# Second layer's selective scan: the input load split in two, dt's sum and u's product moved to GpSimd, the chain that makes u started two groups earlier

## The chip, the core and the metric

The kernel runs on one core of a Trainium2 chip. The metric is the device time of one launch in microseconds (us). Five engines work side by side, each through its own list of instructions: TensorE (PE, with its weight loads shown as PEld), VectorE (DVE), ScalarE (ACT), GpSimd (POOL) and SyncE (SP), which here only issues DMAs. They order themselves by semaphores.

## The reference, cut to what matters

Two layers on an input of 4 images x 128 channels x 64 x 64. Layer 0 is attention with a layer norm; the change does not touch it. Layer 1 adds a 3x3 convolution, a 1x1 convolution between a Fourier transform and its inverse, and a Mamba block over the 4096 positions of each image:

```python
xi, z = split(u @ in_proj)                       # 256 channels each
xs = silu(causal_conv1d(xi, 4 taps) + conv1d_b)
x_dbl = xs @ x_proj.T                            # 8 (for dt) + 16 (B) + 16 (C)
dt = softplus(x_dbl[:8] @ dt_proj.T + dt_proj_b)
h  = exp(dt * A) * h + dt * B * xs               # 256 channels x 16 states
y  = sum_over_states(h * C) + xs * D
ym = (y * silu(z)) @ out_proj.T
out = conv3x3(x) + irfft2(mix(rfft2(x))) + ym
```

## The kernel before

Layer 0 leaves its output in `z_ext` in memory, with a halo of 64 zeros on both sides of each image. Layer 1 (`layer1`) cuts the 4 x 4096 positions into 32 iterations (`NIT`) of 512 positions. In an iteration the 4096 pairs of channel and state are 32 groups (`G`) of 128 rows, and each group is one scan of 128 x 512. The first two iterations are unrolled; the other 30 are 15 passes of a hardware loop (L848) whose body holds two iterations. SyncE's list is unrolled throughout.

There is no scheduler. Each engine has an `emit(it, p)`, which goes through the groups g = 0 to 31 of iteration `it`, and a `prepare(j, p, g)`, which puts a piece of the preparation of the next iteration j = it + 1 behind the work of group g. The numbers in `if g == ...` set where each piece stands in its engine's list. An engine meets them when it comes there, and waits there if the semaphore isn't up.

For each group:

- SP (`load_dt`, L884) loads the group's dt rows from memory, each row repeated for 16 states, into one of 16 buffers `d_a`, when the scan 16 groups earlier is done. It reads them from `dt_dram`, to which `store_dt` (L878) has written the iteration's dt; `store_dt` stands at t = 16 of SP's list and waits for `dt_sum`.
- ACT (`decay`, L1113) makes exp(dt A) in place; `last_state` (L1106) keeps the last state of group g - 6, so ACT is at most six groups ahead of the scans.
- PE (`repeat_u`, L1016) spreads u = dt x over 128 rows into one of four banks; it waits for the scan four groups back, so PE is at most that far ahead.
- DVE multiplies the bank by B (`times_b`, L1181, one group ahead) and scans (L1195). The scan waits for POOL to be done with the state buffer of eight groups earlier.
- POOL multiplies the states by C (`hc`, L1224), and PE sums four groups of them over the states (`sum_states`, L999).

Twice an iteration DVE adds the skip term (`add_skip`, L1166, at g = 21 and, for the iteration before, g = 5) and POOL multiplies by the gate (L1215).

The preparation: `load` brings the 512 positions with their halo to `za` (for the taps, the gate and the Fourier part), the same again to a padded image `zp` (for the 3x3 convolution), and the mirrored rows to `stage_j`. All three count on the semaphore `z_in`, and PE's taps (L935, g = 1 to 7) and ACT's flip (L1066, g = 3) wait for all of them. `load(it + 2)` stands at t = 26 of SP's list and waits for `z_used`, which PE raises when it has used `zp` and `zj` of iteration `it`, the last of the output products of `fill` (at g = 28). From the taps follow silu (g = 10), `xd` (PE g = 11 and 12, ACT g = 15), dt's product (PE g = 15 and 16), Relu and Abs (ACT g = 19 and 20), Exp and Ln (g = 21 and 22, semaphore `sp_log`); then on DVE the sum dt (L1154, g = 20) and the product ux = dt xs (L1157, g = 21, semaphore `u_prod`), then ACT's `high` (L1059) and DVE's `low` (L1148, g = 25 and 26), which split ux into two parts that add up to it, as PE's fast number format needs.

The code that the change touches is printed here with the line numbers of the profile.

Of the kernel before, what the change touches and what calls it, by code (L numbers as in the profile page):

```python
# [8 lines left out]
ALU = mybir.AluOpType  # L9
AX = mybir.AxisListType  # L10

B, C, H, W = 4, 128, 64, 64
# [664 lines left out]
LC = 512  # L677
# [7 lines left out]
def layer1(nc, z_ext, w, out, nb=B):  # L685
# [16 lines left out]
    with ExitStack() as ctx:  # L702
# [59 lines left out]
        with nc.Block() as block:  # L762
# [27 lines left out]
            def _(dve):  # L790
# [23 lines left out]
        (z_in, flipped, item, item_read, sp_log, dt_sum, u_prod, hi_ready, lo_ready,  # L814
         u_rep, da_ready, bu_ready, scanned, kept, hc_ready, y_done, y_added, gated, z_used, o_ready, o_copied,
         o_full, o_even, o_odd, dt_stored) = [sem(x) for x in (
             "z_in", "flipped", "item", "item_read", "sp_log", "dt_sum", "u_prod",
# [35 lines left out]
        with nc.Block() as block:  # L853
            @block.sync
            def _(sp):
                def load(j, p):

                    jw = j % NIT
                    b, lc = jw // STEPS, jw % STEPS

                    ge(sp, z_used, j - 1)
                    ge(sp, flipped, 2 * j)
                    sp.dma_start(za[:, p, :], z_ext[b, :, bass.ds(lc * LC, HALO)]).then_inc(z_in, 16)
                    sp.dma_start(zp[:, p, :, 1:W + 1], z_ext[b, :, bass.ds(lc * LC, HALO)].rearrange("c (h w) -> c h w", w=W)).then_inc(z_in, 16)
# [3 lines left out]
                    sp.dma_start(stage_j[:, ROWS - 1, :], z_ext[b, :, bass.ds((STEPS - lc) % STEPS * LC + W, W)]).then_inc(z_in, 16)  # L868

# [17 lines left out]
                def emit(it, p):  # L887
                    for t in range(G):
# [10 lines left out]
                        if t == 26 and it + 2 <= NIT:  # L899
                            load(it + 2, p)  # L900

                load(0, 0)
                load(1, 1)
# [11 lines left out]
                sp.wait_ge(z_in, 64 * (NIT + 1))  # L915

            @block.tensor
            def _(pe):
# [7 lines left out]
                def prepare(j, p, g):  # L926

                    if 1 <= g <= 7:
                        if g == 1:
                            pe.wait_ge(z_in, j * 64 + 64)  # L930
# [8 lines left out]
                    elif g in (11, 12):  # L939
                        i = g - 11  # L940
# [7 lines left out]
                    elif g in (15, 16):  # L948
                        n = DT + g - 15
# [3 lines left out]
                        nc.tensor.matmul(bank(n), wdt[:, 128 * (g - 15):128 * (g - 15) + 128], xd[:, :], start=True, stop=True  # L953
                                         ).then_inc(item, 1)
                    elif g in (19, 20):
                        n = BI + g - 19
                        begin(j, n)
                        nc.tensor.matmul(bank(n), (sel_b, sel_c)[g - 19][:, :], xd[:, :], start=True, stop=True).then_inc(item, 1)
# [59 lines left out]
                FILLS = (18, 21, 21, 24, 24, 25, 26, 27, 27, 28)  # L1018

                def emit(it, p):  # L1020
                    for g in range(G):
# [4 lines left out]
                        if g in (13, 14) and not (isinstance(it, int) and it == 0):  # L1026
                            out_proj(it - 1, g - 13)
# [283 lines left out]
```

## Time and profile before

| | |
|---|---|
| median of 3 runs | 6187.24 us (6182.13 to 6188.05) |
| profiled execution | 6181.0 us, span 6179.2 us |
| layer 1's scans, first start to last start | 4006.8 to 6163.3 us of the span |
| busy over the span | PE 90%, DVE 79%, POOL 67%, ACT 60% |
| busy from 4006 to 6164 us | DVE 2022.24, PE 1659.10, POOL 1495.03, ACT 1328.44 of 2158 us |

The last row is the one to read: the shares over the whole span mix two layers. The profiled execution is one run; its times are used for sums, and the medians for comparison.

### The profile page before, as it was taken

Reading aid. Unit: us, or ns where it says so; the run is one execution under the profiler, and the core shown is the slowest. Engines: PE = TensorE matmul, PEld = TensorE weight load, DVE = VectorE, ACT = ScalarE, POOL = GpSimd, SP = SyncE. Lnnn points to the kernel's source line nnn. Section 1 sums busy time; section 2 is a strip of 40 time slices with the busy share of each in tenths; the row PEclk is TensorE's granted clock in tenths of the full one; section 3 lists DMA queues with packets and bytes.
Section 4 is the critical chain, followed back from the end, with each engine's and each line's share of the span. In section 5 each row is a group of like instructions: output and inputs, shape, how many; then the busy total and the mean of one; then the engine's idle time right before and its main releaser. Section 6 shows DMA issues by size and latency. Waiting matters only on the chain. (4 is left out here: it accounts for less than half of the span.)

```text
span 6179.2 us, 90944 instructions
## 1 busy us (share of the span) xinstructions
PE 5589.3 (90%) x27184; PEld 2550.2 (41%) x27184; DVE 4912.2 (79%) x7188; ACT 3717.1 (60%) x7290; POOL 4118.1 (67%) x3147
## 2 busy tenths in 40 slices
PE   7999999999999999999999999677777777777777
PEld 3444444444444444444444444233333333333332
DVE  7777777777777777777777777299999999999998
ACT  3666666666656666666666666566566656666665
POOL 2677766676766677666677776376676666676776
PEclk9999999999999999999999999899899889988998
DMA  4011011111110110110100000244444444444444
GB/s 132 20 42 40 29 31 34 32 43 30 32 35 25 38 42 29 40 33 23 31 18 12 21 9 21 67 164 144 157 150 143 153 151 148 142 157 149 146 153 144
DMA packets 293852, 465.18 MB, mean 75 GB/s; under 512 B 73680, under 2 KB 97104, under 8 KB 291920
## 3 DMA queue, kind: packets, MB, share of 16 engines
q1 hardware_dynamic: 293360, 459.70, 23.4%
q8 instruction: 177, 2.90, 0.2%
q14 instruction: 315, 2.58, 0.1%
HBM read 381.74 MB, written 76.28 MB: 74 GB/s over the span
## 5 line engine op out<-in xcount | busy, mean ns | idle before, releaser
L560 POOL TENSOR_TENSOR sums<-exps 128x512 f32<-128x512 f32 x2048 | 2617.3, 1299 | 1312.5 <-ACT exps L493 1307.8
L569 DVE TENSOR_REDUCE mpart<-ps 128x1 f32<-128x512 f32 x4096 | 2539.7, 682 | 820.3 <-PE ps L369 820.3
L493 ACT ACTIVATE exps<-ps 128x512 f32<-128x512 f32 x4096 | 2127.9, 603 | 1405.0 <-PE ps L376 1404.6
L1224 POOL TENSOR_TENSOR hc<-hh,c_rep 128x512 f32<-128x512 f32 x1024 | 1422.0, 1393 | 713.1 <-DVE hh L1195 710.7
L369 PE MATMUL ps<-k_st,q_ring 96*128 96x512 f32 x4096 | 1754.1, 429 | 18.4 <-DMA k_st<-qk_split 9.3
L376 PE MATMUL ps<-q_ring,k_st 98*128 98x512 f32 x4096 | 1621.4, 397 | 4.0 <-ACT exps L493 3.6
L1195 DVE TENSOR_TENSOR_SCAN hh<-d_a,carry,ps 128x512 f32<-128x512 f32 x1024 | 1296.0, 1268 | 1.0
L369 PEld LDWEIGHTS ps<-k_st,q_ring 96*128 96x128 f32 x4096 | 774.6, 189 | 1065.0 <-DVE mpart L569 548.7
L387 PE MATMUL ps<-exps,v_ring 128*32 128x512 f32 x8192 | 1090.8, 605 | 0.0
L1016 PE MATMUL ps<-s_u,sel_g 128*128 128x512 f32 x1024 | 665.6, 650 | 232.6 <-DVE hh L1195 230.5
L376 PEld LDWEIGHTS ps<-q_ring,k_st 98*128 98x128 f32 x4096 | 778.3, 190 | 148.2 <-ACT exps L493 17.3
L1181 DVE TENSOR_TENSOR ps<-ps,b_rep 128x512 f32<-128x512 f32 x1024 | 690.6, 677 | 137.1 <-issue 69.7
L1113 ACT ACTIVATE d_a<-d_a,a_neg 128x512 f32<-128x512 f32 x1024 | 732.0, 720 | 85.8 <-issue 79.7
L1016 PEld LDWEIGHTS ps<-s_u,sel_g 128*128 128x128 f32 x1024 | 210.1, 205 | 832.6 <-DVE hh L1195 671.6
L399 PE MATMUL ps<-sums,ones_d 128*32 128x512 f32 x4096 | 533.1, 592 | 0.0
L935 PE MATMUL ps<-za,wtap 128*128 128x512 f32 x528 | 333.5, 732 | 187.9 <-DMA stage_j<-z_ext 187.9
L999 PE MATMUL ps<-hc,sel_y 128*32 128x512 f32 x2048 | 299.2, 658 | 108.7 <-DVE yt L1166 102.4
L1106 ACT COPY carry<-hh 128x1 f32 (+1 forms) x1024 | 187.5, 183 | 304.6 <-DVE hh L1195 303.8
L387 PEld LDWEIGHTS ps<-exps,v_ring 128*32 128x32 f32 x8192 | 161.2, 108 | 416.3 <-ACT exps L493 361.5
L981 PE MATMUL ps<-zp,wconv 128*128 128x512 f32 x576 | 297.4, 627 | 0.0
L399 PEld LDWEIGHTS ps<-sums,ones_d 128*32 128x32 f32 x4096 | 133.0, 110 | 306.6 <-issue 298.1
L935 PEld LDWEIGHTS ps<-za,wtap 128*128 128x128 f32 x528 | 119.3, 233 | 288.8 <-issue 243.8
(106 smaller groups left out, 2906.1 us busy)
## 6 DMA issues: line engine op xcount, KB each, us to landing
d_a<-dt_dram SPq DMA_DIRECT2D x1040, 256.0 KB
qk_split<-hilo SPq DMA_DIRECT2D x128, 256.0 KB, 2.3
q_ring<-qk_split SPq DMA_DIRECT2D x384, 64.0 KB, 2.0
k_st<-qk_split SPq DMA_DIRECT2D x45, 512.0 KB, 7.0
dt_dram<-dt SPq DMA_DIRECT2D x33, 512.0 KB, 2.8
za<-z_ext SPq DMA_DIRECT2D x33, 320.0 KB, 6.1
zp<-z_ext SPq DMA_DIRECT2D x33, 320.0 KB, 8.0
xc<-in_x SPq DMA_DIRECT2D x32, 256.0 KB, 3.1
```

What stands on the lines that cost most here:

```text
L369: nc.tensor.matmul(d_bank(("max", m, t)), q_ring[0:PARTS, m % 4, 128 * i:128 * i + 128], k_st[0:PARTS, g % 2, chunk(kc)], start=True, stop ...
L376: nc.tensor.matmul(a_bank(("exp", n, t)), k_st[0:SHIFT, n // NCH % 2, 128 * t:128 * t + 128], q_ring[0:SHIFT, n % 4, :], start=True, stop= ...
L387: ins = nc.tensor.matmul(ps[D * i:D * i + D, OUT_BANK, :], v_ring[:, n // NCH % 2, 4 * v + i, :], exps[:, (2 * v + i // 2) % 4, CH * (i % ...
L399: nc.tensor.matmul(ps[D * j:D * j + D, DEN_BANK, :], ones_d[:, :], sums[:, u % 8, :], start=(v == 1), stop=(v == QUADS - 1)).then_inc(sum_ ...
L493: nc.scalar.activation(exps[:, u % 4, CH * half:CH * half + CH], a_bank(("exp", n, t)), ACT.Exp, scale=SCALE).then_inc(a_done, 1)
L560: pool.tensor_tensor(sums[:, u % 8, :], exps[:, u % 4, 0:CH], exps[:, u % 4, CH:2 * CH], ALU.add).then_inc(summed, 1)
L569: nc.vector.tensor_reduce(mpart[:, m % 2, t % 4, t // 4:t // 4 + 1], d_bank(("max", m, t)), AX.X, ALU.max).then_inc(d_done, 1)
L1016: nc.tensor.matmul(ps[:, U_BANK + g % NU, :], sel_g[:, j, :], s_u[:, p, s, :], start=True, stop=True).then_inc(u_rep, 1)
L1113: nc.scalar.activation(d_a[:, g % NDA, :], d_a[:, g % NDA, :], ACT.Exp, scale=a_neg[:, s * 8 + j:s * 8 + j + 1]).then_inc(da_ready, 1)
L1181: nc.vector.tensor_tensor(bu, bu, b_rep[:, p, :], ALU.mult).then_inc(bu_ready, 1)
L1195: nc.vector.tensor_tensor_scan(hh[:, g % NHH, :], d_a[:, g % NDA, :], ps[:, U_BANK + g % NU, :], carry[:, it % STEPS, s * 8 + j:s * 8 + j ...
L1224: pool.tensor_tensor(hc[:, g % NHC, :], hh[:, g % NHH, :], c_rep[:, p, :], ALU.mult).then_inc(hc_ready, 1)
```

## The change

- `load` no longer fills `zp`. It stands at t = 6 of SP's list instead of t = 26 and waits for the last product that reads `za` (`item`), which was made an iteration earlier. `load_padded(it + 1)` fills `zp` at t = 8, on a semaphore of its own, `zp_in`, for which PE waits only at the first output product.
- dt's sum and ux stand on GpSimd, at g = 18 and 19, behind the `hc` product of that group. DVE's list has neither.
- The chain that makes u: silu at ACT g = 9, `xd` at PE 10 and 11 and ACT 13, dt's product at PE 14 and 15, Relu and Abs at ACT 17 and 18, Exp and Ln at 19 and 20, b and c at 21 and 22, `high` and `low` at 23 and 24. The gate's silu moves from 29 to 27.
- The output products (`FILLS`) stand at g = 17 to 27, `out_proj` at 12 and 13, `output` at 16.

```diff
-                def load(j, p):
-                    jw = j % NIT
-                    b, lc = jw // STEPS, jw % STEPS
-                    ge(sp, z_used, j - 1)
+                def load(j):
+                    p, b, lc = j % 2, j % NIT // STEPS, j % STEPS
+                    if j >= 2:
+                        sp.wait_ge(item, (j - 2) * NITEM + GI + 1)
                     ge(sp, flipped, 2 * j)
                     sp.dma_start(za[:, p, :], z_ext[b, :, bass.ds(lc * LC, HALO)]).then_inc(z_in, 16)
-                    sp.dma_start(zp[:, p, :, 1:W + 1], z_ext[b, :, bass.ds(lc * LC, HALO)].rearrange("c (h w) -> c h w", w=W)).then_inc(z_in, 16)
...
+                def load_padded(j):
+                    p, b, lc = j % 2, j // STEPS, j % STEPS
+                    ge(sp, z_used, j - 1)
+                    sp.dma_start(zp[:, p, :, 1:W + 1], z_ext[b, :, bass.ds(lc * LC, HALO)].rearrange("c (h w) -> c h w", w=W)).then_inc(zp_in, 16)
...
-                        if t == 26 and it + 2 <= NIT:
-                            load(it + 2, p)
+                        if t == 6 and it + 2 <= NIT:
+                            load(it + 2)
+                        if t == 8 and it + 1 < NIT:
+                            load_padded(it + 1)
...
# PE
-                            pe.wait_ge(z_in, j * 64 + 64)
+                            pe.wait_ge(z_in, j * 48 + 48)
...
-                    elif g in (15, 16):
-                        n = DT + g - 15
+                    elif g in (14, 15):
+                        n = DT + g - 14
...
                             ge(pe, o_copied, it)
+                            pe.wait_ge(zp_in, it * 16 + 16)
...
-                FILLS = (18, 21, 21, 24, 24, 25, 26, 27, 27, 28)
+                FILLS = (17, 20, 21, 21, 23, 25, 25, 26, 27, 27)
...
# ACT
-                        act.wait_ge(z_in, j * 64 + 64)
+                        act.wait_ge(z_in, j * 48 + 48)
+                        ge(act, z_used, j - 1)
...
-                    elif g == 22:
+                    elif g == 20:
                         act.wait_ge(sp_log, j * 2 + 1)
                         nc.scalar.activation(edt[:, :, :], edt[:, :, :], ACT.Ln, bias=1.0).then_inc(sp_log, 1)
...
-                    elif g in (25, 26):
                         act.wait_ge(u_prod, j + 1)
-                        high(j, p, s_u, ux, g - 25)
+                        high(j, p, s_u, ux, g - 23)
...
# DVE
-                    if g == 20:
-                        dve.wait_ge(sp_log, j * 2 + 2)
-                        nc.vector.tensor_tensor(dt[:, :, :], dt[:, :, :], edt[:, :, :], ALU.add).then_inc(dt_sum, 1)
-                    elif g == 21:
-                        dve.wait_ge(dt_sum, j + 1)
-                        nc.vector.tensor_tensor(ux[:, :, :], dt[:, :, :], xs[:, p, :, :], ALU.mult).then_inc(u_prod, 1)
-                    elif g in (25, 26):
-                        low(j, p, s_u, ux, g - 25)
+                    if g in (23, 24):
+                        low(j, p, s_u, ux, g - 23)
...
# POOL
+                def prepare(j, p, g):
+                    if g == 18:
+                        pool.wait_ge(sp_log, j * 2 + 2)
+                        pool.tensor_tensor(dt[:, :, :], dt[:, :, :], edt[:, :, :], ALU.add).then_inc(dt_sum, 1)
+                    elif g == 19:
+                        pool.wait_ge(dt_sum, j + 1)
+                        pool.tensor_tensor(ux[:, :, :], dt[:, :, :], xs[:, p, :, :], ALU.mult).then_inc(u_prod, 1)
...
                         pool.tensor_tensor(hc[:, g % NHC, :], hh[:, g % NHH, :], c_rep[:, p, :], ALU.mult).then_inc(hc_ready, 1)
+                        prepare(it + 1, 1 - p, g)
```

How the lists stand, where it matters. First GpSimd, the first iteration and a half of layer 1 before; `hc` is the product with C, `yt` the gate:

```order
L1224 TENSOR_TENSOR hc<-hh,c_rep 128x512 x23
L1215 TENSOR_TENSOR yt<-yt,gz 128x512
L1224 TENSOR_TENSOR hc<-hh,c_rep 128x512 x16
L1215 TENSOR_TENSOR yt<-yt,gz 128x512
L1224 TENSOR_TENSOR hc<-hh,c_rep 128x512 x16
```

The same place of the same engine in the changed kernel:

```order
L1223 TENSOR_TENSOR dt<-dt,edt 128x1024
L1226 TENSOR_TENSOR ux<-dt,xs 128x1024
L1235 TENSOR_TENSOR hc<-hh,c_rep 128x512 x19
L1223 TENSOR_TENSOR dt<-dt,edt 128x1024
L1235 TENSOR_TENSOR hc<-hh,c_rep 128x512
L1226 TENSOR_TENSOR ux<-dt,xs 128x1024
L1235 TENSOR_TENSOR hc<-hh,c_rep 128x512 x3
L1218 TENSOR_TENSOR yt<-yt,gz 128x512
```

Two products of double width now stand close together, three `hc` ahead of the gate. Next VectorE, before, from the scan of g = 19 on (`yt` is the skip term):

```order
L1195 SCALAR_TENSOR_TENSOR hh<-d_a,carry,ps 128x512
L1181 TENSOR_TENSOR ps<-ps,b_rep 128x512
L1195 SCALAR_TENSOR_TENSOR hh<-d_a,carry,ps 128x512
L1154 TENSOR_TENSOR dt<-dt,edt 128x1024
L1181 TENSOR_TENSOR ps<-ps,b_rep 128x512
L1195 SCALAR_TENSOR_TENSOR hh<-d_a,carry,ps 128x512
L1157 TENSOR_TENSOR ux<-dt,xs 128x1024
L1166 SCALAR_TENSOR_TENSOR yt<-xs,cols,ps 128x512
L1181 TENSOR_TENSOR ps<-ps,b_rep 128x512
```

VectorE in the changed kernel, from the scan of g = 21 on:

```order
L1198 SCALAR_TENSOR_TENSOR hh<-d_a,carry,ps 128x512
L1169 SCALAR_TENSOR_TENSOR yt<-xs,cols,ps 128x512
L1184 TENSOR_TENSOR ps<-ps,b_rep 128x512
L1198 SCALAR_TENSOR_TENSOR hh<-d_a,carry,ps 128x512
L1184 TENSOR_TENSOR ps<-ps,b_rep 128x512
L1198 SCALAR_TENSOR_TENSOR hh<-d_a,carry,ps 128x512
L1157 TENSOR_TENSOR s_u<-ux,s_u 64x2x512
L1184 TENSOR_TENSOR ps<-ps,b_rep 128x512
L1198 SCALAR_TENSOR_TENSOR hh<-d_a,carry,ps 128x512
L1157 TENSOR_TENSOR s_u<-ux,s_u 64x2x512
```

`low` (`s_u`, which is L1157 in the changed kernel) stands two groups behind the skip term, where it stood four behind. Last SyncE's queue, an iteration before, from one `load` to the next:

```order
L863 DMA za<-z_ext 128x640
L864 DMA zp<-z_ext 128x10x64
L867 DMA stage_j<-z_ext 128x448
L868 DMA stage_j<-z_ext 128x64
L884 DMA d_a<-dt_dram 128x1x512 x21
L878 DMA dt_dram<-dt 128x2x512
L884 DMA d_a<-dt_dram 128x1x512 x3
L873 DMA out<-o_sb 128x512
L884 DMA d_a<-dt_dram 128x1x512 x8
```

SyncE's queue in the changed kernel:

```order
L862 DMA za<-z_ext 128x640
L865 DMA stage_j<-z_ext 128x448
L866 DMA stage_j<-z_ext 128x64
L888 DMA d_a<-dt_dram 128x1x512 x2
L872 DMA zp<-z_ext 128x10x64
L888 DMA d_a<-dt_dram 128x1x512 x7
L882 DMA dt_dram<-dt 128x2x512
L888 DMA d_a<-dt_dram 128x1x512 x3
L877 DMA out<-o_sb 128x512
L888 DMA d_a<-dt_dram 128x1x512 x20
```

The loads of z stand 20 groups' dt loads ahead of where they were.

## Rows read from the trace of the kernel before

**Rows 1.** Busy time over layer 1: length, then each engine, clock, DMA share.
```profile
4006.00:6164.00 2158.00, 1659.10 (x5618) 673.08 (x5616) 2022.24 (x2270) 1328.44 (x2782) 1495.03 (x1086) 0.90 0.46 151
```

**Rows 2.** VectorE in layer 1, by line: busy, mean ns, idle before, releasers.
```profile
L1195 DVE TENSOR_TENSOR_SCAN hh<-d_a,carry,ps 128x512 f32<-128x512 f32 x1024 | 1296.0, 1268 | 1.0
L1181 DVE TENSOR_TENSOR ps<-ps,b_rep 128x512 f32<-128x512 f32 x1024 | 690.6, 677 | 137.1 <-issue 69.7 <-PE ps L1016 66.1
L1148 DVE TENSOR_TENSOR s_u<-ux,s_u 64x1024 fp32r<-64x1024 f32 x64 | 78.1, 1220 | 2.0
L1166 DVE SCALAR_TENSOR_TENSOR yt<-xs,cols,ps 128x512 f32<-128x512 f32 x64 | 46.7, 730 | 3.4 <-PE ps L999 3.4
```

**Rows 3.** VectorE in order of time: start, us, line, [idle before].
```profile
4623.93 1.26 DVE L1195 TENSOR_TENSOR_SCAN hh<-d_a,carry,ps 128x512 f32<-128x512 f32 x1
...
4639.85 1.26 DVE L1195 TENSOR_TENSOR_SCAN hh<-d_a,carry,ps 128x512 f32<-128x512 f32 x1
...
4647.06 1.26 DVE L1195 TENSOR_TENSOR_SCAN hh<-d_a,carry,ps 128x512 f32<-128x512 f32 x1
4648.25 1.19 DVE L1154 TENSOR_TENSOR dt<-dt,edt 128x1024 f32<-128x1024 f32 x1
...
4649.97 1.26 DVE L1195 TENSOR_TENSOR_SCAN hh<-d_a,carry,ps 128x512 f32<-128x512 f32 x1
4651.16 1.19 DVE L1157 TENSOR_TENSOR ux<-dt,xs 128x1024 f32<-128x1024 f32 x1
...
4658.84 1.26 DVE L1195 TENSOR_TENSOR_SCAN hh<-d_a,carry,ps 128x512 f32<-128x512 f32 x1
...
4661.99 1.28 DVE L1195 TENSOR_TENSOR_SCAN hh<-d_a,carry,ps 128x512 f32<-128x512 f32 x1
```

**Rows 4.** VectorE at two iteration ends: the loop's own (4677), the one inside (4612).
```profile
4612.04 0.70 DVE L1181 TENSOR_TENSOR ps<-ps,b_rep 128x512 f32<-128x512 f32 x1 [2.48 <-PE ps L1016]
4677.83 1.30 DVE L1181 TENSOR_TENSOR ps<-ps,b_rep 128x512 f32<-128x512 f32 x2 [4.92 <-issue]
4681.17 0.70 DVE L1181 TENSOR_TENSOR ps<-ps,b_rep 128x512 f32<-128x512 f32 x1 [0.86 <-PE ps L1016]
```

**Rows 5.** TensorE's taps behind the load, in order of time.
```profile
4678.63 2.07 PE L935 MATMUL ps<-za,wtap 128*128 128x512 f32 x2 [8.10 <-DMA stage_j<-z_ext]
4688.35 1.02 PE L935 MATMUL ps<-za,wtap 128*128 128x512 f32 x2
```

**Rows 6.** Stretches around the wait for z; columns as in rows 1.
```profile
4664.00:4672.00 8.00, 4.00 (x24) 1.98 (x22) 7.97 (x10) 1.39 (x4) 5.66 (x5) 1.00 0.82 205
4680.00:4684.00 4.00, 4.00 (x8) 1.76 (x6) 2.89 (x5) 2.80 (x7) 2.15 (x2) 0.50 0.44 163
```

**Rows 7.** SyncE's queue in order of time.
```profile
4664.92 6.14 SPq L867 DMA_DIRECT2D stage_j<-z_ext  x1
```

**Rows 8.** The loop's branch (L848), one taken: queue, count, duration, start.
```profile
L848 DVEq COMPARE_BRANCH  x1: 63/63/63, 4670.8 to 4670.8; - x1
L848 POOLq COMPARE_BRANCH  x1: 45/45/45, 4673.0 to 4673.0; - x1
L848 POOLq FUSED_REGOPS  x1: 59/59/59, 4673.3 to 4673.3; - x1
L848 DVEq FUSED_REGOPS  x1: 74/74/74, 4677.6 to 4677.6; - x1
```

**Rows 9.** GpSimd in layer 1: the C product (min/median/max ns), then beside VectorE's dt.
```profile
L1224 POOL TENSOR_TENSOR hc<-hh,c_rep x1024: 1256/1276/2326, 4008.1 to 6164.7; 128x512 f32<-128x512 f32 x171
4648.49 2.09 POOL L1224 TENSOR_TENSOR hc<-hh,c_rep 128x512 f32<-128x512 f32 x1 [0.58 <-DVE hh L1195]
4657.35 2.49 POOL L1224 TENSOR_TENSOR hc<-hh,c_rep 128x512 f32<-128x512 f32 x2
```

**Rows 10.** Layer 0: VectorE products of two SBUF tensors, and GpSimd beside one.
```profile
L633 DVE TENSOR_TENSOR scaled<-centred,rstd x32: 692/830/1769, 865.9 to 3948.3; 128x512 f32<-128x512 f32 x32
1098.58 2.69 POOL L560 TENSOR_TENSOR sums<-exps 128x512 f32<-128x512 f32 x2 [2.77 <-ACT exps L493]
1100.05 1.77 DVE L633 TENSOR_TENSOR scaled<-centred,rstd 128x512 f32<-128x512 f32 x1
```

**Rows 11.** ScalarE in layer 1: `high` by line, and its wait (total us, times, longest).
```profile
L1059 ACT CAST s_u<-ux 64x1024 fp32r<-64x1024 f32 x64 | 66.8, 1044 | 177.4 <-DVE ux L1157 176.6
ACT s_u L1059 <- DVE ux L1157: 176.6, 32, 5.6
```

More of the change, by code:

```diff
@@ L812, in layer1 @@
         clear(nc, names)
-        (z_in, flipped, item, item_read, sp_log, dt_sum, u_prod, hi_ready, lo_ready,
+        (z_in, zp_in, flipped, item, item_read, sp_log, dt_sum, u_prod, hi_ready, lo_ready,
          u_rep, da_ready, bu_ready, scanned, kept, hc_ready, y_done, y_added, gated, z_used, o_ready, o_copied,
          o_full, o_even, o_odd, dt_stored) = [sem(x) for x in (
-             "z_in", "flipped", "item", "item_read", "sp_log", "dt_sum", "u_prod",
+             "z_in", "zp_in", "flipped", "item", "item_read", "sp_log", "dt_sum", "u_prod",
              "hi_ready", "lo_ready", "u_rep", "da_ready", "bu_ready", "scanned", "kept", "hc_ready", "y_done",
@@ L898, in emit @@
                             store(it - 1, 1 - p)
-                        if t == 26 and it + 2 <= NIT:
-                            load(it + 2, p)
-                load(0, 0)
-                load(1, 1)
+                        if t == 6 and it + 2 <= NIT:
+                            load(it + 2)
+                        if t == 8 and it + 1 < NIT:
+                            load_padded(it + 1)
+                load(0)
+                load_padded(0)
+                load(1)
                 store_dt(0, 0)
@@ L938, in prepare @@
                                 ins.then_inc(item, 1)
-                    elif g in (11, 12):
-                        i = g - 11
+                    elif g in (10, 11):
+                        i = g - 10
                         if i == 0:
@@ L947, in prepare @@
                             ins.then_inc(item, 1)
-                    elif g in (15, 16):
-                        n = DT + g - 15
+                    elif g in (14, 15):
+                        n = DT + g - 14
                         begin(j, n)
                         pe.wait_ge(item_read, j * NITEM + XD + 1)
-                        nc.tensor.matmul(bank(n), wdt[:, 128 * (g - 15):128 * (g - 15) + 128], xd[:, :], start=True, stop=True
+                        nc.tensor.matmul(bank(n), wdt[:, 128 * (g - 14):128 * (g - 14) + 128], xd[:, :], start=True, stop=True
                                          ).then_inc(item, 1)
-                    elif g in (19, 20):
-                        n = BI + g - 19
+                    elif g in (18, 19):
+                        n = BI + g - 18
                         begin(j, n)
-                        nc.tensor.matmul(bank(n), (sel_b, sel_c)[g - 19][:, :], xd[:, :], start=True, stop=True).then_inc(item, 1)
+                        nc.tensor.matmul(bank(n), (sel_b, sel_c)[g - 18][:, :], xd[:, :], start=True, stop=True).then_inc(item, 1)
                     elif g in (22, 23):
@@ L1025, in emit @@
                             sum_states(it - 1, 6 + g // 4)
-                        if g in (13, 14) and not (isinstance(it, int) and it == 0):
-                            out_proj(it - 1, g - 13)
+                        if g in (12, 13) and not (isinstance(it, int) and it == 0):
+                            out_proj(it - 1, g - 12)
                         for n in range(10):
@@ L1123, in emit @@
                         prepare(it + 1, 1 - p, g)
-                        if g == 17 and not (isinstance(it, int) and it == 0):
+                        if g == 16 and not (isinstance(it, int) and it == 0):
                             output(it - 1, 1 - p)
```

19 lines of the change are left out of this document (10 added, 9 removed).

## The prediction

> **What bounds the kernel now.** I read first the busy time over layer 1 alone, since the page's shares mix the two layers. In 2158 us VectorE is busy 2022 and TensorE 1659, GpSimd 1495 and ScalarE 1328 [rows 1]. So VectorE sets the time, and idles some 136 us. The lines of VectorE say where: the scans wait for nothing (1.0 us in 1024), and all idle time, 137.1 us, stands before `times_b`, 66.1 us of it put down to TensorE and 69.7 to "issue", a wait that the profile can't name [rows 2].
>
> Next the time of one group. From the scan at 4623.93 to the one at 4639.85 there are nine groups, 15.92 us, 1.77 each [rows 3]. 1024 groups make 1811 us. The rest of VectorE's busy time, some 208 us or 6.5 an iteration, is dt, ux, `low`, skip and row. An iteration is therefore 63.1 us of work and 4.3 of waiting.
>
> The waits all fall on the change of iteration, and there are two kinds [rows 4]. Inside the loop body VectorE waited 2.48 us for TensorE. TensorE stood before its first tap, 8.10 us in the case shown, until the DMA of z had landed [rows 5], and behind that tap stand the copies of u for the next groups. The third DMA of that load had been issued only at 4664.92, and held SyncE's queue for 6.14 us [rows 7], because `load` waits for the last output product; between it and the tap lie three or four groups. The pause costs a second time: the clock granted to TensorE is 0.50 in the stretch behind it (1.2 of 2.4 GHz) and two passes of a tap take 2.07 instead of 1.02 us [rows 5, 6], so VectorE waits again (0.86 us at 4681.17 [rows 4]).
>
> At the loop's own end VectorE waits 4.92 us for "issue" [rows 4]. The branch explains it: VectorE's sequencer branches at 4670.8 and its next instruction comes at 4677.6, 6.8 us later, while GpSimd goes on 0.3 us after its branch [rows 8]. VectorE has to get its instructions again; 1.9 us of that are covered by scans already handed over. Of 15 passes 14 branch back, so 69.7 us are 14 halts of 5.0. (The Trainium skill, Runtime: NRT & Kernel Launch, section Instruction fetch mechanics, says that a taken branch to a target outside the engine's small window of instructions forces a DMA fetch before the engine goes on. The trace agrees for VectorE and not for GpSimd, whose body is shorter. Since it is a DMA, this halt doesn't go with the wait for z.)
>
> **The change, part by part.**
>
> *The load of z at t = 6.* Its condition, a product of the iteration before, is long true, and the flip it also needs is done at g = 3. It is needed at the next g = 1, 27 groups or 48 us later, against 13.7 us from 4664.92 [rows 7] to the tap at 4678.63 [rows 5]. The wait for z goes whole. What is left of TensorE's 66.1 us is its slow clock behind the loop's halt, where TensorE can still only run four groups ahead: I keep 0.6 us at each of 14, 8 us. **-58 us.** Queued behind the early load on SyncE are dt loads for 16 groups later. ScalarE wants them 10 groups (17.7 us) after their issue at the earliest, and a hold of 6.14 us [rows 7] fits in that. `zp` has from t = 8 to g = 17 of the next iteration. Both are costed at nothing; if that cover were gone, each us late beyond 17.7 would cost 32 us.
>
> *dt and ux off VectorE.* With dt between, two scans are 2.91 us apart instead of 1.77, so dt costs 1.14, and ux is of the same size (1.19 us both) [rows 3]. 2 x 1.14 x 32 = **-73 us**.
>
> *The same on GpSimd.* No row shows a 128x1024 product there. Two of 128x512 back to back take 2.49 us [rows 9], which I take. The bounds are 1.27 (one of half the width) and 4.65 (twice 2.33, the slowest `hc`, held up by VectorE [rows 9]). GpSimd then has 1495 + 32 x 5.0 = 1655 us of work, below VectorE's, so only the place matters. I count from the end of scan 18. GpSimd: `hc` to 1.35, dt to 3.85, `hc` to 5.1, ux to 7.6. ScalarE has Ln ready by then: Ln stands at its g = 20, which it can reach after scan 14, seven us before. `high` takes 1.05 [rows 11] and ends at 8.75. VectorE ends scan 23 at 5 x 1.77 + 0.7 (the skip term [rows 2]) = 9.5 and does `low`, 1.22 us [rows 2]. So u comes 0.75 us before it is wanted, and ScalarE, which now waits longer for ux than its 5.6 us of before [rows 11], gives exp for scan 24 at 9.6 us, against 11.5 wanted. Nothing lost here.
>
> *What `low` meets.* This is the price of the move. A VectorE product of two SBUF tensors and GpSimd's products hold each other up. Beside dt, `hc` took 2.09 us instead of 1.28 [rows 9]. Before, GpSimd always lost, since dt, ux and `low` start the moment a scan ends, just ahead of `hc`. Layer 0 shows the other order: a product of 0.69 us took 1.77 when it started, at 1100.05, inside GpSimd's two that ran from 1098.58 to 1101.27 [rows 10]. It waited 1.08 us, until GpSimd was done. (The Trainium skill, SBUF — State Buffer, section Who interferes with whom, has it as a rule: the two share a port pair, whoever starts first keeps it for the instruction and the other blocks fully. The rows agree, and the rule speaks against leaving a queue of GpSimd work where `low` stands.) That queue is what the change makes. GpSimd goes on with `hc` 20 to 8.85 and `hc` 21 to 10.1; `low` is due at 9.5 and waits 0.6, to end at 11.3. `hc` 22 and the gate run to 13.8; scan 24 ends at 13.1 and the second `low` waits 0.7. That is 1.3 us an iteration, **+42 us**; from both sides 0 and 2 x 1.25 x 32 = 80. The products C that come late are wanted by TensorE's sums one to three us before it could stall VectorE, and by the scans eight groups on: nothing.
>
> *The loop's halt.* Before, ScalarE's and VectorE's fetch fell into the load of z, with the DMA engines busy 0.82 of the time [rows 6]; now they meet only dt loads. No row shows a fetch without z. Bounds: the 5.0 us of now, and none, as on GpSimd. I take 3.5 us, nearer to what is seen. 14 x (5.0 - 3.5) = **-21 us**.
>
> *Before the first scan* dt and ux are on the path, each 1.25 us longer: **+2.5 us**. Splits, fills and the earlier chain cost nothing by themselves: they fill time in which TensorE (1659 of 2158 us) and ScalarE (1328) wait for scans.
>
> **Sum.** -58 - 73 + 42 - 21 + 2.5 = -107.5 us. Against the profiled execution's 6181.0 us that is 6073.5, against the median 6187.2 it is 6080. I forecast **6076 us**.
>
> **The rivals.**
>
> *Less in the way* (15%). The fetch is hidden without z, or `low` hits gaps. For: the bounds above. Without halts 6076 - 49 = 6027, without port waits 6034. Against: the 14 halts make 69.7 us in all, so they hardly vary around 5.0.
>
> *Starved* (12%). The first `low` gets the port only when GpSimd has nothing left. Against: in [rows 10] VectorE got it at the next end. Then it waits for `hc` 20 to 22, the gate and `hc` 23, from 9.5 to 7.6 + 5 x 1.25 = 13.85; 4.35 instead of 1.3 us an iteration, 6076 + 98 = 6174. A milder case of the same group, the dt loads held up by z, would give back the 58 us: 6134.
>
> *GpSimd too slow* (the other side, 6%). If one wide product takes P us, ux ends at 2.6 + 2P, and `low` waits from P = 2.9 on, 2 us an iteration for each us of P. The gain is gone, and 0.2% more lost, when 64 (P - 2.9) = 107 + 12, at P = 4.8. That is just above twice the slowest `hc`; at P = 5.5 it would be 6076 + 166 = 6242. Against: VectorE's scans and `times_b` run beside `hc` at 1.27 us without holding it up.
>
> *The change does nothing* (4%). Something hidden under the wait for z, such as the fetch or the slow clock, takes its whole place, and the port takes the 73 us back: 6187.
>
> **Numbers.** The forecast's case has 63%, and its own range is 6045 to 6110 (halt 2 to 5 us, port waits 0.5 to 2). The range for 8 in 10 is 6020 to 6140. A difference of 0.2%, 12 us, is about what a measurement here can tell. Faster: 63 + 15 + 12 = 90, less 1 for a starved case that is worse than drawn; same 4; slower 7.
>
> **What would show it.** TensorE's first tap without a wait for z, and no 8 us pause of TensorE; VectorE's idle time before `times_b` down from 137 to some 57, almost all "issue"; `low` at some 1.85 us mean instead of 1.22; wide products on GpSimd of 2.5 us; the loads of z at t = 6 with the dt loads behind them in time. I'd be wrong if `hi_ready` were late at `low`, if VectorE waited for exp or for the state buffers, or if the fetch took longer than before.

## The result and the profile after

The changed kernel took **6036.98 us** (median of 4 runs, 6034.72 to 6038.47), against 6187.65 us for the kernel before (4 runs, 6182.13 to 6198.22). The ratio is 0.9754, with a 95% interval from 0.9737 to 0.9771. The profiled spans are 6035.0 and 6179.2 us. The forecast was 6076 us, in a range of 6020 to 6140.

The stretch of layer 1 comes first, in the columns of [rows 1]: length, busy time and instructions of PE, PEld, DVE, ACT and POOL, granted clock, DMA share, GB/s.

```profile
4010.00:6020.00 2010.00, 1610.13 (x5615) 642.23 (x5613) 1952.07 (x2204) 1309.20 (x2780) 1581.78 (x1150) 0.95 0.47 162
```

VectorE still sets the time. It now works 1952 of 2010 us, where it worked 2022 of 2158 [rows 1]. TensorE's clock in the layer is 0.95 instead of 0.90.

VectorE by line in the same layer (busy, mean ns, idle before, releasers), which answers to [rows 2]:

```profile
L1198 DVE TENSOR_TENSOR_SCAN hh<-d_a,carry,ps 128x512 f32<-128x512 f32 x1024 | 1298.1, 1270 | 1.1
L1184 DVE TENSOR_TENSOR ps<-ps,b_rep 128x512 f32<-128x512 f32 x1024 | 690.5, 677 | 59.6 <-issue 52.2 <-PE ps L1024 6.4
L1157 DVE TENSOR_TENSOR s_u<-ux,s_u 64x1024 fp32r<-64x1024 f32 x64 | 87.1, 1361 | 2.0
```

The idle time fell from 137.1 to 59.6 us; the part put down to TensorE fell from 66.1 to 6.4, and "issue" from 69.7 to 52.2. `low` takes 1361 ns instead of 1220. The prediction had named some 57 us of idle time, almost all of it "issue", and some 1.85 us for `low`.

From first to last scan start, layer 1 lasts 2009.8 us (4009.58 to 6019.36) instead of 2156.6. I laid the distances between scans side by side, group by group. The sums over 32 iterations show where the 146.8 us went (all in us):

| place | measured | forecast |
|---|---|---|
| change of iteration: wait for z and loop's halt | -85.5 | -58 - 21 |
| groups 20 and 21: dt and ux gone from VectorE | -72.6 | -73 |
| groups 23 to 26: `low` waits for the port | +9.1 | +42 |
| group 28 waits for TensorE | +2.2 | 0 |
| before the first scan (outside the 146.8) | +2.8 | +2.5 |

In the changes of iteration, the 15 inside the loop body lost 3.59 us on the mean over the plain 1.77-us pitch; now they lose 0.00. The 14 at the loop's end lost 5.66 and now lose 3.85. The rest is the iterations ahead of the loop.

How the 85.5 us divide between z and the halt needs one more view, because "issue" in the kernel before isn't the branch alone. VectorE's waits in both kernels (total us, times, longest):

```profile
DVE ps L1181 <- issue: 69.7, 21, 4.9
DVE ps L1184 <- issue: 52.2, 14, 3.8
```

Of the 21 waits before, the 14 behind the branch make 64.6 us, 4.61 each, and seven of about 0.7 us come some 12 us behind it; these are gone with the early load. So the halt gave back 64.6 - 52.2 = 12.4 us, and the wait for z with what hangs on it 73.

### The profile page after: what moved, and what is told of

It is laid out like the page before. It is cut to its first block and busy times, and to the rows that moved or that the text cites. A ratio compares the mean times of both kernels' runs of the same rounds, so it can differ in the third digit from the quotient of the medians.

```text
span 6035.0 us, 91036 instructions
## 1 busy us (share of the span) xinstructions
PE 5545.1 (92%) x27184; PEld 2521.5 (42%) x27184; DVE 4842.5 (80%) x7122; ACT 3699.3 (61%) x7290; POOL 4212.8 (70%) x3213
## 5 line engine op out<-in xcount | busy, mean ns | idle before, releaser
L1235 POOL TENSOR_TENSOR hc<-hh,c_rep 128x512 f32<-128x512 f32 x1024 | 1363.3, 1339 | 438.2 <-DVE hh L1198 436.1
L1024 PE MATMUL ps<-s_u,sel_g 128*128 128x512 f32 x1024 | 586.5, 574 | 247.5 <-DVE hh L1198 246.7
L1184 DVE TENSOR_TENSOR ps<-ps,b_rep 128x512 f32<-128x512 f32 x1024 | 690.5, 677 | 59.6 <-issue 52.2
L989 PE MATMUL ps<-zp,wconv 128*128 128x512 f32 x576 | 316.0, 652 | 0.0
L942 PE MATMUL ps<-za,wtap 128*128 128x512 f32 x528 | 284.4, 634 | 27.0 <-DMA stage_j<-z_ext 27.0
L1067 ACT CAST s_u<-ux 64x1024 fp32r<-64x1024 f32 x66 | 69.0, 1045 | 283.5 <-POOL ux L1226 282.7
```

Source lines behind the costliest of these rows:

```text
L1024: nc.tensor.matmul(ps[:, U_BANK + g % NU, :], sel_g[:, j, :], s_u[:, p, s, :], start=True, stop=True).then_inc(u_rep, 1)
L1184: nc.vector.tensor_tensor(bu, bu, b_rep[:, p, :], ALU.mult).then_inc(bu_ready, 1)
L1235: pool.tensor_tensor(hc[:, g % NHC, :], hh[:, g % NHH, :], c_rep[:, p, :], ALU.mult).then_inc(hc_ready, 1)
```

## The experiments

All times are medians; every ratio is against the kernel before in runs on the same chip, whose median there was 6193.8 us for the old load, the load alone, dt on VectorE and dt's sum at 17, 6183.8 for the second run of the changed kernel, `low` at 27, `zp` at 29 and the written-out kernel, and 6183.7 for the other four. The changed kernel, run again beside the later ones, is the reference:

> The changed kernel once more beside the others of this set, as their reference: 6037 us.

It took 6036.1 us (6034.06 to 6037.18; 0.9761, 0.9748 to 0.9775).

### The load and its place

**The early load alone.** The kernel before with the split early load and nothing else: DVE's dt and ux, the fills and the chain stand as before.

> The kernel before with the split load alone (za and mirrored rows at t = 6, zp at t = 8); dt and ux stay on VectorE, the chain and the products stay where they were. Theory (the wait for z and its after-effects cost 85 us, and nothing is hidden under them): 6187 - 85 = 6102 us, with VectorE's halt at the loop's end down from 5.0 to 3.7 us as in the changed kernel. Rival (under the wait for z lies another one, such as u's two halves that come at g = 25 and 26 or the fetch of instructions, so that the load needs the rest of the change): at most half of it, 6145 us or more.

Measured: 6097.52 us (0.9841, 0.9825 to 0.9858). The theory holds: the load is worth 96 us by itself there by the medians and 86 by the profiles' layer (2156.6 and 2070.4), and the halt is 3.67 us. Between this kernel and the changed one lie 57 us of span (6092.2 and 6035.0).

**The changed kernel with the old load.**

```diff
-                        if t == 6 and it + 2 <= NIT:
-                            load(it + 2)
-                        if t == 8 and it + 1 < NIT:
-                            load_padded(it + 1)
+                        if t == 26 and it + 2 <= NIT:
+                            load(it + 2, p)
...
```

`load` and the counts on `z_in` are those of the kernel before.

> The changed kernel with the load of z as it was: one load of za, zp and the mirrored rows at t = 26, waiting for the last output product, one semaphore. Everything else as changed, so the output products end one group earlier (27) than in the kernel before. Theory (the load came late because it waited for the last output product, and each group that this ends earlier takes 1.77 us off the wait): the early load is worth the 85 us that the scans behind the iteration's change lost before, and 32 x 1.77 = 57 of them come from the order alone; so 28 us above the changed kernel's 6037, 6065 us. Rival (the order of the products gives nothing, since the DMA's own queue sets when z lands): the whole 85 us come back, 6122 us.

Measured: 6155.83 us (0.9930, 0.9913 to 0.9947), 119 us above the changed kernel by the medians and 127.6 by the profiles' layer (the profiled execution was the longest of the four). Neither number was near. Here is one change of iteration, TensorE, VectorE and SyncE's queue in order of time:

```profile
4661.53 8.94 SPq L884 DMA_DIRECT2D d_a<-dt_dram  x7
4663.22 1.02 PE L984 MATMUL ps<-zj,wmix 128*128 128x512 f32 x2
4668.60 1.27 DVE L1189 TENSOR_TENSOR_SCAN hh<-d_a,carry,ps 128x512 f32<-128x512 f32 x1
4670.56 0.40 SPq L863 DMA_DIRECT2D za<-z_ext  x1
4671.49 4.86 SPq L867 DMA_DIRECT2D stage_j<-z_ext  x1
```

The last output product (L984) was done at 4664.2. The load came 6 us later, right behind scan 26 (4668.60 to 4669.87), since a dt load that waits for this scan stands ahead of it in SyncE's list. So my forecast had the load waiting for the wrong thing: finishing the products a group earlier gives nothing. And the move of `low` made the old load dearer. `low` at 25 and 26 put VectorE work behind the load's place, which gave the DMA time; at 23 and 24 that time is gone. It is one `low`, 1.40 us of distance between scans, in each of 31 iterations: 43 us on top of the 85.5 for the waits, together 129. The distances bear it out: the changes of iteration lose 1.34 us more than in the kernel before inside the body and 1.31 at the loop's end, and those ahead of the loop 6 us together.

**The kernel before with the load one group earlier.**

```diff
-                        if t == 26 and it + 2 <= NIT:
+                        if t == 25 and it + 2 <= NIT:
```

> The kernel before with one number changed: load at t = 25 of SyncE's list instead of t = 26, everything else as it was. Theory (the load was late because of its place behind scan 26, not because of the last output product: in the trace the product ends at 4661.2 and the load is issued at 4663.97, right behind the scan of g = 26): z is asked for when the product is done, some 2.7 us earlier, and VectorE's loss at the waits for z, 66 us, goes nearly whole; the halts at the loop's end stay at 5 us. 6187 - 60 = 6127 us. Rival (the prediction's: the load waits for the last output product, so that its place in the list is nothing): 6187 us.

Measured: 6155.23 us (0.9956, 0.9943 to 0.9970), 28 us faster than before with one number changed. That settles what released the load in the kernel before: the place. But only half of the gain came. SyncE's queue and TensorE in order of time, in this kernel:

```profile
4655.27 1.02 PE L984 MATMUL ps<-zj,wmix 128*128 128x512 f32 x2
4656.32 0.32 SPq L863 DMA_DIRECT2D za<-z_ext  x1
4657.15 6.98 SPq L867 DMA_DIRECT2D stage_j<-z_ext  x1
4669.93 2.07 PE L935 MATMUL ps<-za,wtap 128*128 128x512 f32 x2 [3.21 <-DMA stage_j<-z_ext]
```

The product ends at 4656.29 and the load starts at 4656.32: now the product is the limit, close behind the other. And from the load's issue to the tap it takes 13.6 us here (4656.32 to 4669.93), and 14.0 us on the mean of the 29 changes of iteration in the loop, where the kernel before took 12.4. The third DMA of the load holds SyncE's queue longer too, 6.6 us on the mean against 5.0, which fits an earlier load that meets more of the dt loads; no run separates that. The tap still runs at the slow clock (2.07 us for two passes, as in [rows 5]).

### GpSimd, VectorE and their common port

GpSimd and VectorE of the changed kernel in order of time, one iteration (start, us, line):

```profile
4671.83 2.36 POOL L1223 TENSOR_TENSOR dt<-dt,edt 128x1024 f32<-128x1024 f32 x1
4675.37 2.37 POOL L1226 TENSOR_TENSOR ux<-dt,xs 128x1024 f32<-128x1024 f32 x1
4677.69 4.73 POOL L1235 TENSOR_TENSOR hc<-hh,c_rep 128x512 f32<-128x512 f32 x3
4680.05 1.23 DVE L1157 TENSOR_TENSOR s_u<-ux,s_u 64x1024 fp32r<-64x1024 f32 x1
4682.38 1.28 POOL L1218 TENSOR_TENSOR yt<-yt,gz 128x512 f32<-128x512 f32 x1
4683.24 1.50 DVE L1157 TENSOR_TENSOR s_u<-ux,s_u 64x1024 fp32r<-64x1024 f32 x1
```

The second `low` starts inside GpSimd's gate product, which ends at about 4683.6, waits 0.28 us for it, and then takes its 1.22. The first one comes just as a C product ends and waits for nothing: the record is 1.23 us long. This repeats in all 32 iterations to some hundredths of a us.

**dt and ux back on VectorE, at g = 18 and 19.**

```diff
 # DVE
-                    if g in (23, 24):
+                    if g == 18:
+                        dve.wait_ge(sp_log, j * 2 + 2)
+                        nc.vector.tensor_tensor(dt[:, :, :], dt[:, :, :], edt[:, :, :], ALU.add).then_inc(dt_sum, 1)
+                    elif g == 19:
+                        dve.wait_ge(dt_sum, j + 1)
+                        nc.vector.tensor_tensor(ux[:, :, :], dt[:, :, :], xs[:, p, :, :], ALU.mult).then_inc(u_prod, 1)
+                    elif g in (23, 24):
...
 # POOL
-                        prepare(it + 1, 1 - p, g)
```

> The changed kernel with dt's sum and u's product back on VectorE, at the same g = 18 and 19. Theory (the move is worth VectorE's 2.26 us an iteration less 0.28 of port wait at the second low product and 0.07 at g = 28): 32 x 1.91 = 61 us more than 6037, 6098 us, and low at 1.22 us again. Rival (GpSimd's load costs the scans in other ways too, through late C products, and the move gains less): under 6085 us.

Measured: 6096.82 us (0.9839, 0.9822 to 0.9855). The total is right, but its parts aren't those I gave. Between scans, dt and ux cost 72.6 us. The first `low` waits 0.62 us even without wide products on GpSimd (+20), since GpSimd, held up by these products and by the gate, is still catching up with C products; the second waits for nothing (-9). The loss at the loop's end falls from 3.85 to 2.37 us (-21), and group 28 is free (-2). These, rounded, make +60.6, and the layer is 61.0 longer.

This kernel also shows what the earlier chain is worth. It differs from the one with the early load alone (6097.52 us, layer 2070.4) by the chain that starts two groups earlier and the output products, and takes 6096.82 us, layer 2070.7: nothing in total. The shorter halt (-21) and the port wait of the first `low` (+20) cancel.

**dt's sum one group earlier on GpSimd.**

```diff
-                    if g == 18:
+                    if g == 17:
```

> The changed kernel with dt's sum on GpSimd one group earlier, at g = 17; ux stays at 19. One number, no work more or less. Theory (a VectorE product of two SBUF tensors that meets a GpSimd product already running waits to its end, and only by luck of phase does low wait 0.0 and 0.28 us in the changed kernel): counted from the end of scan 18, ux then ends at 6.7, the products C run from 6.7 in steps of 1.24, low is due at 9.5 and waits to 10.4, and the second one waits for the gate or a product C behind it, together about 1.6 us an iteration instead of 0.3: 41 us more, 6078 us. Rival (an earlier start of GpSimd's work can only help, and low waits for nothing): 6037 us or less.

Measured: 6042.10 us (0.9747, 0.9731 to 0.9764). GpSimd and VectorE in order of time:

```profile
4614.42 3.73 POOL L1235 TENSOR_TENSOR hc<-hh,c_rep 128x512 f32<-128x512 f32 x3
4617.33 1.91 DVE L1157 TENSOR_TENSOR s_u<-ux,s_u 64x1024 fp32r<-64x1024 f32 x1
4618.12 2.24 POOL L1218 TENSOR_TENSOR yt<-yt,gz 128x512 f32<-128x512 f32 x1
```

`low` now starts 0.8 us ahead of the end of a C product and waits 0.69 (1.91 less 1.22): +22 us over 32 iterations, from the order alone. GpSimd's next instruction then waits for `low`, 2.24 us instead of 1.28. VectorE had the port when the running product ended, although GpSimd had more in its queue, so the "starved" rival of the prediction is excluded here (the next run has the exception). Of the 41 us forecast, 22 came as port wait, since the second `low` waits no longer than before, and the halt gave 13 us back (below), so that the total is 5 us above the changed kernel: a miss in size. The distances between scans show the mechanism.

**`low` four groups later, at g = 27 and 28.**

> The changed kernel with low on VectorE at g = 27 and 28 instead of 23 and 24; high stays. Theory (by g = 27 GpSimd has caught up, its products start behind the scan as low does and lose the port to it): the 0.28 us at the second low product go, 32 x 0.28 = 9 us, perhaps the 2 us at g = 28 as well: 6027 us, low at 1.22 us. Rival (u's second half then comes too late for TensorE's first copies of the next iteration): a new wait before the first products with B, 6037 us or more.

Measured: 6047.49 us (0.9781, 0.9767 to 0.9794), a miss of the sign. I had thought that GpSimd would have caught up by g = 27. VectorE's `low` by line:

```profile
L1157 DVE TENSOR_TENSOR s_u<-ux,s_u 64x1024 fp32r<-64x1024 f32 x64 | 98.2, 1534 | 2.0
```

It had not: the distance behind scan 27 is 3.81 us on the mean (median 3.51, up to 4.77), where a group with `low` alone takes 3.16. The second, at 28, waits for nothing.

The spread holds something that the other runs don't show. In all but one of the 32 iterations the first `low` starts 0.44 to 0.48 us ahead of the end of a C product. In 24 iterations it gets the port at that end and waits about 0.3 us. In the other 8 GpSimd's next C product goes first, and `low` waits 1.54 to 1.58 us. One of each, VectorE and GpSimd:

```profile
4434.57 1.54 DVE L1157 TENSOR_TENSOR s_u<-ux,s_u 64x1024 fp32r<-64x1024 f32 x1
4430.06 7.18 POOL L1235 TENSOR_TENSOR hc<-hh,c_rep 128x512 f32<-128x512 f32 x5
4495.76 2.80 DVE L1157 TENSOR_TENSOR s_u<-ux,s_u 64x1024 fp32r<-64x1024 f32 x1
4491.26 6.23 POOL L1235 TENSOR_TENSOR hc<-hh,c_rep 128x512 f32<-128x512 f32 x5
```

In the first case one of GpSimd's five products waits for `low` (7.18 us for the five); in the second none does (6.23 us). So a waiting VectorE product doesn't always get the port at the next end. What decides is not shown. It is still far from "starved": that rival had `low` wait for all of GpSimd's queue, 4.35 us.

### The loop's halt

**The changed kernel with the loop written out.** All engines' lists of layer 1 become straight code; SyncE's was so already.

```diff
-            with e.Fori(1, NIT // 2) as k:
-                for r in range(2):
-                    emit(k * 2 + r, r)
+            for it in range(2, NIT):
+                emit(it, it % 2)
```

> The changed kernel with layer 1's loop written out: 30 iterations in a row in each engine's list, no branch. Theory (the wait named issue is the fetch behind the taken branch, and straight code is fetched ahead): the 14 halts of 3.7 us go, 52 us less, 5985 us; VectorE's idle time before its products with B under 8 us. Rival (a list of 15 times the length has to be fetched all the same, and that costs here and there what the branch cost): 6037 us.

Measured: 5986.87 us (0.9683, 0.9670 to 0.9697). VectorE's `times_b` by line:

```profile
L1183 DVE TENSOR_TENSOR ps<-ps,b_rep 128x512 f32<-128x512 f32 x1024 | 701.3, 688 | 12.6 <-PE ps L1023 11.6
```

"issue" is gone. So the 52.2 us were the branch, as the prediction had it. The idle time left, 12.6 us, is above the 8 that I named; TensorE's sum at group 28 has a part in it (8.6 us in the distances, see below).

**The same in the kernel before.**

> The kernel before with layer 1's loop written out. Theory (at the loop's end the fetch and the wait for z lay side by side, and without the fetch the wait for z of the other iterations, 2.5 us, is left): 14 x 2.5 = 35 us less, 6152 us. Rival (the halts of 5.0 us were apart from z): 70 us less, 6117 us.

Measured: 6159.93 us (0.9963, 0.9951 to 0.9975), 24 us for the same edit that was worth 50 above (6037 to 5987). Its `times_b`:

```profile
L1180 DVE TENSOR_TENSOR ps<-ps,b_rep 128x512 f32<-128x512 f32 x1024 | 691.2, 678 | 112.0 <-PE ps L1015 110.6
```

Without the halt VectorE stands before z instead: 110.6 us put down to TensorE, where it was 66.1 [rows 2]. The fetch and the load ran side by side, and neither could be removed alone for its full share. In the distances at the changes of iteration the early load gives 86 us with the halt still there and 114 without the loop; writing out the loop gives 26 us with the late load and 54 with the early one. Of my 35 us the loop's ends gave 31, and the changes inside the body, which wait for z a little longer, took 5 back.

**`zp` loaded at t = 29,** so that a load of z runs beside the fetch again, and nothing waits for it.

```diff
-                        if t == 8 and it + 1 < NIT:
+                        if t == 29 and it + 1 < NIT:
```

> The changed kernel with the load of the padded image zp at t = 29 instead of t = 8, in time for its first use at g = 17 of the next iteration, so that it runs while VectorE fetches its instructions at the loop's end. Theory (the fetch is a DMA that queues with the data's, which is why the halt fell from 5.0 to 3.7 us when the load of z moved away): the halt goes back to some 5 us, 14 x 1.3 = 18 us more, 6055 us. Rival (the fetch has its fixed time, and the halt fell for another reason): 6037 us, halt 3.7 us.

Measured: 6061.05 us (0.9803, 0.9790 to 0.9816):

```profile
L1198 DVE TENSOR_TENSOR_SCAN hh<-d_a,carry,ps 128x512 f32<-128x512 f32 x1024 | 1308.6, 1281 | 13.8 <-issue 12.7
L1184 DVE TENSOR_TENSOR ps<-ps,b_rep 128x512 f32<-128x512 f32 x1024 | 700.8, 687 | 73.2 <-issue 64.8 <-PE ps L1024 7.4
```

The 64.8 us of "issue" over 14 branches are 4.63 us each, against 3.73 in the changed kernel and 4.61 in the kernel before: a load beside the fetch makes the halt longer, by as much as it had become shorter. That is 12.6 us. The other 12.7 us stand before a scan some 12 us behind each branch, where the kernel before has its seven short waits. I hadn't forecast them, and no run shows what they are; together they make the 25 us, against 18 forecast.

The sequencer's own rows give the same. VectorE's branch (L848) in the changed kernel, duration in ns and start:

```profile
L848 DVEq COMPARE_BRANCH  x1: 63/63/63, 4629.5 to 4629.5; - x1
L848 DVEq FUSED_REGOPS  x1: 74/74/74, 4635.2 to 4635.2; - x1
```

From the branch to the next instruction it is 5.7 us here and was 6.8 in [rows 8]. Means of the 14 branches, with the DMA engines' busy share in the 4 us behind:

| kernel | branch to next instruction, us | DMA share |
|---|---|---|
| before | 6.50 | 0.69 |
| changed, `zp` at t = 29 | 6.52 | 0.79 |
| changed | 5.61 | 0.53 |
| changed, dt's sum at g = 17 | 4.69 | 0.47 |
| changed, dt and ux on VectorE | 4.05 | 0.44 |

From kernel to kernel the fetch takes longer the busier the DMA engines are; within one kernel they go together in some (`zp` at t = 29, dt's sum at 17) and not in others (before, the changed one). Where dt is summed earlier, the dt loads are through earlier, which fits the shorter halts of the last two rows; I made no run of that alone. By these rows the move of dt to GpSimd has a price that the prediction didn't name, a longer halt (21 us against dt on VectorE). (The Trainium skill, Runtime: NRT & Kernel Launch, section Instruction fetch mechanics, has a taken branch out of the instruction window fetch its target by DMA; the rows of this table fit it.) GpSimd goes on 0.27 us after the same branch in each of these kernels.

### Towards a better version

**Written out, `low` at g = 28 and 29.**

```diff
-                    if g in (23, 24):
-                        low(j, p, s_u, ux, g - 23)
+                    if g in (28, 29):
+                        low(j, p, s_u, ux, (28, 29).index(g))
```

> The changed kernel with layer 1's loop written out (5987 us) and low at g = 28 and 29. Theory (at 27 GpSimd had not caught up, and the first low waited 0.65 us on the mean; two groups on it has, and its products start behind the scan as low does and lose the port to it; and GpSimd's products are no longer held up at 23 and 24, so TensorE's sum at g = 28 comes in time): the 9 us of port waits and the 8 us at g = 28 go, 5970 us. Rival (GpSimd is held up elsewhere, or u's second half is late for TensorE's first copies of the next iteration): 5987 us or more.

Measured: **5975.69 us** (0.9664, 0.9651 to 0.9677), the fastest of all, and 61 us below the changed kernel. Its `low` by line:

```profile
L1156 DVE TENSOR_TENSOR s_u<-ux,s_u 64x1024 fp32r<-64x1024 f32 x64 | 78.1, 1220 | 2.0
```

No port wait is left. Against `low` at 23 and 24 in the written-out kernel, that is -8.8 us (64 times 1.357 less 1.220), and -8.6 at group 28; against it stand +4.8 at group 0, where u now comes 0.15 us late each time.

**Written out, `low` at g = 23 and 25.**

> The changed kernel with the loop written out and low at g = 23 and 25, the second one a group later. Theory (what low waits is set by where in GpSimd's back-to-back products it comes, to a tenth of a us): the second low is due 14.5 us after the end of scan 18 and GpSimd's product ends at 14.6, so it waits 0.1 instead of 0.28: 6 us less, 5981 us. Rival (the wait comes with the backlog, not with the phase): 5987 us.

Measured: 6001.55 us (0.9705, 0.9692 to 0.9718), slower where I forecast faster. GpSimd and VectorE in order of time:

```profile
4673.02 4.71 POOL L1234 TENSOR_TENSOR hc<-hh,c_rep 128x512 f32<-128x512 f32 x3
4674.41 2.19 DVE L1156 TENSOR_TENSOR s_u<-ux,s_u 64x1024 fp32r<-64x1024 f32 x1
```

The second C product began at about 4674.25, `low` came 0.16 us later, and waited 0.97 us for it. A phase read from one trace was right to 0.2 us, and that wasn't enough.

## Why the prediction was right, and what it mis-sized

- **VectorE sets the time, and the wait for z goes whole: right.** Inside the body nothing is left of 3.59 us; the early load alone gives 96 us. The size was low: 58 forecast, 73 measured. Of the 8 us kept for TensorE's slow clock behind the halt 1.6 came, and the 5 us of short waits that went with z had been booked to the halt. SyncE's queue isn't held up by it either, where one DMA took 6.14 us [rows 7]; in the changed kernel:

```profile
4650.29 0.43 SPq L865 DMA_DIRECT2D stage_j<-z_ext  x1
```

- **Why the load was late: wrong reason, right place.** I wrote "because `load` waits for the last output product". It waited for its place behind scan 26 (the load starts 0.70 us after that scan's end each time); the product had ended 2.7 to 4.1 us ahead of the load. The forecast didn't suffer, since the early load clears both. The forecast for the changed kernel with the old load did.
- **dt and ux: -73 forecast, -72.6 measured.** Wide products on GpSimd take 2.36 us (2.49 taken; the bounds were 1.27 and 4.65). The rival "GpSimd too slow", which needed 4.8, is excluded. ScalarE waits longer for ux, as said, and it costs nothing (total us, times, longest; 176.6 and 5.6 in [rows 11]):

```profile
ACT s_u L1067 <- POOL ux L1226: 282.7, 33, 8.8
```

- **The port: the step that was off.** +42 us forecast, +9.1 measured. The mechanism is as drawn: `low` waits out the GpSimd instruction that runs when it comes. The sum took 0.6 and 0.7 us of waits; they are 0.00 and 0.28. I let the wide products take 2.49 us; they are 2.36 and ux ends 0.4 us sooner, so that `low` meets the end of a C product and not its middle. That was luck of phase: shifts of one group put the wait of one `low` anywhere from 0 to 0.97 us. (The Trainium skill, SBUF — State Buffer, section Who interferes with whom, has the block for the length of the instruction. The rows agree on the product that is running; who comes next they show both ways, 24 times to 8 with `low` at g = 27.) By it the port half of the rival "less in the way" nearly came true: without port waits it had 6034 us, and 6037 was measured. The forecast itself, 6076, was 39 us high and its own range, 6045 to 6110, too narrow; only the wide range held.
- **The halt: -21 forecast, -12.4 measured, right in kind.** 3.73 us of "issue" for each branch (52.2 / 14), 3.5 taken. The start was misread: "14 halts of 5.0" took all 69.7 us of 21 waits, of which the longest is 4.9; the 14 behind the branch are 4.61 each. The halt half of the rival "less in the way" needed none, and is excluded.
- **Together.** The terms named make -107.5; the profile has -144 and the medians -150.7. 33 us of the difference are the port, some 6 are that the waits at the changes of iteration were worth 85.5 and not 79; the late C products cost 2.2 at group 28, which I had at nothing. The 6 us between the profile and the medians no term explains; it is the profiled execution of the kernel before, 6181.0 us, that lies below its median.
- **Costed at nothing and not quite so:** the late C products. TensorE's sum waits for them ahead of group 28, and VectorE then for TensorE: 2.2 us, and 8.6 in the written-out kernel. But the wait alone costs nothing. TensorE in the written-out kernel, in two iterations:

```profile
4793.74 1.06 PE L1006 MATMUL ps<-hc,sel_y 128*32 128x512 f32 x8 [2.15 <-POOL hc L1234]
4854.89 1.93 PE L1006 MATMUL ps<-hc,sel_y 128*32 128x512 f32 x8 [2.15 <-POOL hc L1234]
```

The pause is 2.15 us in both. In the first the granted clock stays at 1.00 (2.4 GHz) and group 28 takes its 1.77 us. In the second it is 0.50 behind the pause, the eight products take 1.93 us instead of 1.06, and group 28 takes 0.5 us more. TensorE pauses like that (2.14 to 2.16 us) in 28 of the 32 iterations there, and in 12 of the changed kernel's; in 16 and in 5 of them the clock behind the pause is 0.50, and these are just the iterations with a long group 28. In all the others it is 1.00.

- **Slips in the working.** The forecast's own range doesn't follow from its bounds: halts of 2 to 5 us and port waits of 0.5 to 2 give 6029 to 6119, not 6045 to 6110. The DMA share of 0.82 [rows 6] was read mostly ahead of the branch; in the 4 us behind it the mean is 0.69. The rest of VectorE's work is 211 us (2022 - 1811), not 208. None of these changes the sum.

It stays open why GpSimd's (and TensorE's) branch costs only 0.27 us. VectorE has 432 recorded instructions in the body, ScalarE 337, GpSimd 204, but TensorE some 800, so the count alone doesn't order them.

## What to carry to other kernels

Price a move from VectorE to GpSimd twice: what VectorE saves, which a trace gives to 1%, and what its products of two SBUF tensors wait where they meet GpSimd's back-to-back work, which hangs on tenths of a us; keep both ends of the latter in the range, and move such a product to where GpSimd is idle when a scan ends. When a DMA is late, look both at its semaphore and at what stands ahead of it in the queue's list; here one number (t = 26 to 25) was worth 28 us. Two waits that run side by side, here a load and an instruction fetch, are each worth their full share only once the other is gone: 24 us against 50 for the same edit.

## What the runs showed of the hardware

- A loop branch on VectorE cost 4.05 to 6.6 us from the branch to the next instruction, more with busier DMA engines, and 0.27 on GpSimd; written-out code had no such halt.
- A waiting VectorE product mostly got the port at the end of GpSimd's running instruction, with more GpSimd work queued; in the run with `low` at g = 27 GpSimd's next product went first in 8 of 32 iterations, and the wait was 1.54 to 1.58 us instead of 0.3. Coming 0.16 us behind the start of a GpSimd product cost 0.97 us.
- In the written-out kernel a pause of 2.15 us on TensorE was followed by a granted clock of 0.50 in 16 iterations and of 1.00 in 12; only the first kind cost time, 0.5 us.
- A 128x1024 product of two f32 tensors in SBUF takes 2.36 us on GpSimd and 1.19 on VectorE [rows 3].
